# Moving the product with gamma of a layer norm from VectorE to POOL, with a per-row offset for ScalarE, in a two-layer routed adapter kernel

## Chip, cores and metric

One Trainium2 chip, one of its cores. The metric is the device time of one execution in microseconds (us); the median of several runs counts. Before the change it is 2822.74 us (median of 3 runs, 2821.48 to 2826.43).

## What is computed

128 sequences of 128 rows by 1024 columns, in fp32, go through two adapter layers. In each layer a sequence is given one of the layer's adapters by its token `itok`:

```python
h = gelu(x @ W_down[role] + b_down[role])      # 1024 -> 512, exact gelu
u = h @ W_up[role] + b_up[role]                # 512 -> 1024
y = x + u
mean = jnp.mean(y, axis=-1, keepdims=True)
var = jnp.mean(jnp.square(y - mean), axis=-1, keepdims=True)
yn = (y - mean) * rsqrt(var + 1e-5)
out = yn * gamma[role] + beta[role]            # input of the second layer
```

gamma and beta have 1024 values for each adapter, the same for all rows; mean and var are one number for each row.

## The kernel before

**Steps.** At the start VectorE sorts the 128 sequences by adapter and pairs them, so that both sequences of a pair share their weights: 65 pairs a layer, 130 in all. The kernel is a software pipeline over these pairs, one step for each pair `i`. Step `i` runs on every engine and works on several pairs at once: TensorE multiplies pair `i` with W_down (`down`, L492) and pair `u = i-3` with W_up (`product`, L504); `w = i-2` is the pair whose gelu output is transposed and split; `u-1 = i-4` is the pair that is normalised and stored. Within a pair `e` is 0 or 1, the sequence.

**fp32 by three products.** Each operand is split into a high part (ScalarE copies to the rounded type: `high_x` L603, `high_h` L644, `high_wd` L550, `high_wu` L565) and a low part (VectorE subtracts: `low_x` L812, `low_h` L834, `low_wd` L752, `low_wu` L769); TensorE adds high*high, high*low and low*high. W_up is applied to a pair by seven half-size products instead of eight; their inputs are sums that POOL makes (`sums`, L448 to L453, in `cs`). A step has 48 matmuls of `down` and 42 of `product`, all 128x512, in alternation: product 0, down 0, product 1, down 1, and so on, fifteen pieces of six matmuls.

**What VectorE does in a step.** `begin(i)`: transpose the gelu output `hT` (L819), add products 1 and 2 onto the residual `xt` (`onto`, L844), `low_x` of the second sequence, a new adapter's weights if there is one, `low_h(w, 0)`. `end(i)`: `onto` product 3; `variance(u-1)` (L867), a [128, 2] tile from the sums of squares; `scale(u-1, 0)` (L875); in layer 1 `transpose_x` (L805); `low_h(w, 1)`; `last_onto` product 4 (L852); `scale(u-1, 1)`; `last_onto` 5; `low_x` of the next pair; `last_onto` 6; the mean (L860); `low_h(w, 2)`; `last_onto` 7; the mean; `low_h(w, 3)`. TensorE waits on `s_v`, which counts the additions onto `xt`, before it writes a bank again (product 5 waits for addition 4, product 6 for addition 5), and on `s_wd` and `s_wu`, which VectorE's queue signals when a pair's weights stand ready (`ready`, L796).

**The normalisation.** The work on one sequence `xt[:, k, :]` of 128x1024 passes through three engines, each waiting on a semaphore of the one ahead:

```python
scale:  xt = (xt + nmean) * (gamma * sqrt(H))   # VectorE L875, s_n
norm:   rstd = var ** -0.5                      # POOL L433, [128, 2], s_rs
normal: xt = xt * rstd                          # ScalarE L662, waits s_rs, s_n; gives s_z
shift:  xt = xt + beta                          # POOL L440, waits s_z; gives s_o
store:  DMA to mid or out                       # SyncE L338, waits s_o
```

`nmean` is minus the mean. POOL's order in a step is `sums(w)`, `norm(u-1)`, `take_bu` if w has a new adapter (L408, L410), `shift(u-1, 0)`, `factors` if w has a new adapter (L415, L417, L419, three subtractions of 128x1024), `shift(u-1, 1)`, `take_gb` if u has a new adapter (loads gamma and beta to `cgb` and multiplies gamma by sqrt(H), L427).

**What sets the order.** Every engine's instructions stand in a fixed order in its own queue; nothing is scheduled at run time. The steps are loops of six pairs a turn (`steps` for SyncE, VectorE and ScalarE, `plain_steps` for POOL and TensorE), eight turns in each layer, with some steps written out between and around them. `halves` makes a turn of VectorE end after a `begin` and ahead of an `end`, that is ahead of `onto` product 3.

**New adapters.** Pairs are sorted, so the adapter changes four times in all, the first of these at the start. At the other three `take_wd_0`, `take_wd_1` and `take_wu_0` to `take_wu_2` refill the split weights on ScalarE, VectorE and POOL.

Of the kernel before, what the change touches and what calls it, by code (L numbers as in the profile page):

```python
# [46 lines left out]
def routed_adapters(nc, x, xB, itok, Wd, bd, Wu, bu, ga, be, out):  # L47
# [7 lines left out]
    with ctx:  # L55
# [37 lines left out]
        rstd = sb("rstd", [128, 4])  # L93
        mhalf = sb("mhalf", [128, 1])
# [72 lines left out]
        s_n = sem("s_n")  # L167
# [220 lines left out]
        def _(eng):  # L388
# [40 lines left out]
            def norm(p):  # L429
                if p.exists():  # L430
                    n = 2 * (p.c % 2)
                    count(eng, s_var, p, 1, 1)
                    eng.tensor_tensor(rstd[:, n:n + 2], var[:, n:n + 2], mhalf[:, 0:1].broadcast_to([128, 2]), ALU.pow)\  # L433
                       .then_inc(s_rs, 1)

            def shift(p, e):
                if p.exists():
                    k = p.slot(e)
                    count(eng, s_z, p, 2, e + 1)
                    eng.tensor_tensor(xt[:, k, :], xt[:, k, :], cgb[:, 1, :], ALU.add).then_inc(s_o, 1)  # L440
# [101 lines left out]
        def _(eng):  # L542
# [114 lines left out]
            def normal(p, e):  # L657
                if p.exists():
                    n, k = 2 * (p.c % 2) + e, p.slot(e)
                    count(eng, s_rs, p, 1, 1)  # L660
                    count(eng, s_n, p, 2, e + 1)
                    eng.activation(xt[:, k, :], xt[:, k, :], ACT.Copy, scale=rstd[:, n:n + 1]).then_inc(s_z, 1)  # L662
# [34 lines left out]
        def _(eng):  # L697
# [158 lines left out]
            def mean(u, e, n):  # L856
                if u.exists():
                    b = u.c % 2
                    count(eng, s_v, u, 7, n)
                    eng.tensor_scalar(nmean[:, 2 * b + e:2 * b + e + 1], ys[:, b, 2 * e:2 * e + 1],  # L860
                                      ys[:, b, 2 * e + 1:2 * e + 2], -1.0 / H, ALU.add, ALU.mult).then_inc(s_nm, 1)
# [7 lines left out]

            def scale(u, e):  # L870
                if u.exists():
                    n, k = 2 * (u.c % 2) + e, u.slot(e)
                    count(eng, s_sq, u, 4, 2 * e + 2)
                    count(eng, s_cg, u, 1, 1)
                    eng.scalar_tensor_tensor(out=xt[:, k, :], in0=xt[:, k, :], scalar=nmean[:, n:n + 1],  # L875
                                             in1=cgb[:, 0, :], op0=ALU.add, op1=ALU.mult).then_inc(s_n, 1)
# [14 lines left out]
            def end(i):  # L891
# [4 lines left out]
                scale(u + -1, 0)  # L896
# [5 lines left out]
                scale(u + -1, 1)  # L902
# [47 lines left out]
```

## Time and profile before

| | |
|---|---|
| median of 3 runs | 2822.74 us (2821.48 to 2826.43) |
| the profiled execution's own time | 2828.77 us |
| its span | 2826.8 us |
| instructions | 56889 |
| TensorE matmul busy | 2711.9 us (96%) |
| VectorE busy | 2159.2 us (76%) |
| ScalarE busy | 1689.6 us (60%) |
| POOL busy | 1422.4 us (50%) |
| mean granted TensorE clock | 0.982 of full speed |

The span is the time from the first to the last recorded instruction. Rows of a timeline give the start in us from the span's start, then the duration, the engine, the line of the kernel, the operation, output<-inputs, the shapes and how many; in brackets stands how long the engine was idle just before and what ended that. "PE" is TensorE, "DVE" VectorE, "ACT" ScalarE, "SPq" SyncE's queue, "DVEq" VectorE's queue, which handles waits and signals.

### The profile page before, as it was taken

What the parts mean: (1) busy time and instruction counts of PE and PEld (TensorE: products, weight loads), DVE (VectorE), ACT (ScalarE), POOL (GpSimd) and SP (SyncE); (2) the same over time, 40 slices, a digit from 0 to 9 for tenths busy, and PEclk for the clock granted to TensorE, in tenths of its full rate; (3) what the DMA queues carried; (4) which work ended last, traced back from release to release, by engine and by line L of the source; (5) the groups of instructions that cost most, each with busy time, mean ns of one, the idle gap of its engine ahead of it and who ended that gap; (6) DMA issues with size and microseconds to landing.
All of it is one profiled execution on the core that took longest, in us unless ns stands there. A gap on an engine that the chain in (4) does not pass through costs nothing.

```text
span 2826.8 us, 56889 instructions
## 1 busy us (share of the span) xinstructions
PE 2711.9 (96%) x11714; PEld 2216.2 (78%) x11714; DVE 2159.2 (76%) x3321; ACT 1689.6 (60%) x2907; POOL 1422.4 (50%) x956
## 2 busy tenths in 40 slices
PE   7899999998899999999989999999889999999997
PEld 5688888887788888888768888888667888888885
DVE  4677777766777777777788888888787888888886
ACT  3566666565565656666556565666555655656565
POOL 2455555555555555555454444444354444444446
PEclk9999999999999999999999999999999999999999
DMA  6565666666565656666666666656666666666663
GB/s 186 176 202 191 218 205 210 209 222 212 189 209 195 224 197 211 205 207 206 213 200 212 203 207 196 222 192 215 203 197 205 213 199 202 207 192 219 208 203 146
DMA packets 366261, 574.33 MB, mean 203 GB/s; under 512 B 41216, under 2 KB 241024, under 8 KB 365696
## 3 DMA queue, kind: packets, MB, share of 16 engines
q1 hardware_dynamic: 363968, 563.31, 61.5%
q0 software_dynamic: 1728, 6.29, 0.8%
q14 instruction: 553, 4.53, 0.6%
q8 instruction: 12, 0.20, 0.0%
HBM read 364.97 MB, written 204.47 MB: 201 GB/s over the span
## 4 chain that ended last, share of the span: by engine, by line
PE 82%; issue 7%; DVE 5%; POOL 1%; DVEq 1%; ACT 1%; DMA 1%; SPq 1%; POOLq 1%; ACTq 0%
PE pD L492 44%; PE bX L504 22%; PE bZ L504 16%; DVE xt L852 1%; DVE wul L769 1%; DVEq L222 1%; DVE hl L834 1%; DVE xt L875 1%; DVE wdl L752 0%; DVE xt L844 0%; DMA rwd<-in_Wd 0%; DVE xl L812 0%; POOL rwu L408 0%; POOL rwu L415 0%; ACT wdh L550 0%
## 5 line engine op out<-in xcount | busy, mean ns | idle before, releaser
L440 POOL TENSOR_TENSOR xt<-xt,cgb 128x1024 f32<-128x1024 f32 x260 | 699.8, 2692 | 342.9 <-ACT xt L662 341.6
L492 PE MATMUL pD<-wdh,xh 128*128 128x512 f32 x2080 | 818.9, 394 | 48.8 <-DVEq L796 40.4
L492 PE MATMUL pD<-wdl,xh 128*128 128x512 f32 x2080 | 815.1, 392 | 0.0
L492 PE MATMUL pD<-wdh,xl 128*128 128x512 f32 x2080 | 814.1, 391 | 0.0
L662 ACT ACTIVATE xt<-xt,rstd 128x1024 f32<-128x1024 f32 x260 | 298.9, 1150 | 383.1 <-POOL rstd L433 303.0
L492 PEld LDWEIGHTS pD<-wdh,xh 128*128 128x128 f32 x2080 | 394.6, 190 | 140.9 <-DVEq L796 49.5
L492 PEld LDWEIGHTS pD<-wdh,xl 128*128 128x128 f32 x2080 | 394.0, 189 | 83.0
L492 PEld LDWEIGHTS pD<-wdl,xh 128*128 128x128 f32 x2080 | 394.7, 190 | 81.4
L875 DVE SCALAR_TENSOR_TENSOR xt<-xt,nmean,cgb 128x1024 f32<-128x1024 f32 x260 | 441.4, 1698 | 0.0
L448 POOL TENSOR_TENSOR cs<-hT 128x256 f32<-128x256 f32 x130 | 97.1, 747 | 681.7 <-DVE hT L819 679.2
L504 PE MATMUL bX<-wuh,hh 128*128 128x512 f32 x1040 | 410.8, 395 | 27.7 <-DVE xt L844 21.5
L504 PE MATMUL bX<-wul,hh 128*128 128x512 f32 x1040 | 406.9, 391 | 0.0
L504 PE MATMUL bX<-wuh,hl 128*128 128x512 f32 x1040 | 406.9, 391 | 0.0
L644 ACT ACTIVATE hh<-cs 128x512 fp32r<-128x512 f32 x260 | 163.5, 629 | 369.1 <-PE bX L504 303.1
L654 ACT ACTIVATE pC<-xt,nmean 128x512 f32<-128x512 f32 x520 | 358.2, 689 | 41.5 <-issue 18.0
L433 POOL TENSOR_TENSOR rstd<-var,mhalf 128x2 f32<-128x2 f32 x130 | 217.6, 1674 | 315.6 <-DVE var L867 315.5
L504 PE MATMUL bZ<-wuh,hh 128*128 128x512 f32 x780 | 309.8, 397 | 14.7 <-DVE xt L852 13.2
L834 DVE TENSOR_TENSOR hl<-hT,hh 128x256 fp32r<-128x256 f32 (+1 forms) x260 | 157.9, 607 | 212.6 <-issue 151.9
L504 PE MATMUL bZ<-wul,hh 128*128 128x512 f32 x780 | 308.3, 395 | 0.0
L504 PE MATMUL bZ<-wuh,hl 128*128 128x512 f32 x780 | 308.1, 395 | 0.0
L504 PEld LDWEIGHTS bX<-wuh,hh 128*128 128x128 f32 x1040 | 196.1, 189 | 82.3 <-DVE xt L844 30.7
L834 DVE TENSOR_TENSOR hl<-cs,hh 128x512 fp32r<-128x512 f32 x260 | 190.8, 734 | 79.3 <-issue 78.8
(91 smaller groups left out, 3798.8 us busy)
## 6 DMA issues: line engine op xcount, KB each, us to landing
xq<-in_xB SPq DMA_DIRECT2D x130, 512.0 KB, 3.7
htok<-hg SPq DMA_DIRECT2D x260, 256.0 KB, 2.8
hq<-htok SPq DMA_DIRECT2D x1040, 64.0 KB, 2.3
xt<-in_x SPq DMA_DIRECT2D x130, 512.0 KB, 4.2
mid<-xt SPq DMA_DIRECT2D x130, 512.0 KB, 3.9
xq<-mid SPq DMA_DIRECT2D x520, 128.0 KB, 3.2
xt<-mid SPq DMA_DIRECT2D x130, 512.0 KB, 4.1
out<-xt SPq DMA_DIRECT2D x130, 512.0 KB, 2.7
```

The source lines that it names most:

```text
L222: return eng.value_load(c_new[0:1, bass.ds(p.times(1), 1)], min_val=0, max_val=1)
L433: eng.tensor_tensor(rstd[:, n:n + 2], var[:, n:n + 2], mhalf[:, 0:1].broadcast_to([128, 2]), ALU.pow)\
L440: eng.tensor_tensor(xt[:, k, :], xt[:, k, :], cgb[:, 1, :], ALU.add).then_inc(s_o, 1)
L448: eng.tensor_tensor(cs[:, 0, :], b1, b2, ALU.add).then_inc(s_S, 1)
L492: last = eng.matmul(pD[e][:, :], a[:, e, 128 * k:128 * k + 128], w[:, k, :], start=False, stop=(k == 7 and n == 2), skip_group_check=True)
L504: last = eng.matmul(bank[:, :], a[:, left, 128 * c:128 * c + 128], w[:, n, c, :], start=(start and c == 0 and m == 0), stop=(c == 1 and m ...
L644: eng.activation(dst, src, ACT.Copy).then_inc(s_hh, 1)
L654: eng.activation(junk[:, :], xt[:, u.slot(e), K * m:K * m + K], ACT.Square, bias=nmean[:, n:n + 1], accum_out=ssq[:, b, m, e:e + 1]).then_ ...
L662: eng.activation(xt[:, k, :], xt[:, k, :], ACT.Copy, scale=rstd[:, n:n + 1]).then_inc(s_z, 1)
L769: eng.tensor_tensor(wul[:, n, :, :], block, wuh[:, n, :, :].bitcast(fp32), ALU.subtract)\
L834: eng.tensor_tensor(blocks, src, high.bitcast(fp32), ALU.subtract).then_inc(s_hl, 1)
L875: eng.scalar_tensor_tensor(out=xt[:, k, :], in0=xt[:, k, :], scalar=nmean[:, n:n + 1], in1=cgb[:, 0, :], op0=ALU.add, op1=ALU.mult).then_i ...
```

## The change

`scale` leaves VectorE (two instructions a step, and semaphore `s_n`). ScalarE's `normal` becomes `Identity(xt * rstd + nshift)`, where `nshift = nmean * rstd` is a [128, 2] tile that POOL makes right behind `rstd`; it waits for `s_rs` to reach 2 a pair, and for the squares of its sequence (`s_sq`). POOL's `shift` first multiplies the sequence by gamma (128x1024, counted in `s_g`, which the addition of beta waits for) and then adds beta. VectorE's `mean` waits until the `nshift` that reads the same part of `nmean` is done, two pairs back.

```diff
@@ -432,11 +433,17 @@
                     count(eng, s_var, p, 1, 1)
                     eng.tensor_tensor(rstd[:, n:n + 2], var[:, n:n + 2], mhalf[:, 0:1].broadcast_to([128, 2]), ALU.pow)\
                        .then_inc(s_rs, 1)
+                    count(eng, s_rs, p, 2, 1)
+                    eng.tensor_tensor(nshift[:, n:n + 2], nmean[:, n:n + 2], rstd[:, n:n + 2], ALU.mult)\
+                       .then_inc(s_rs, 1)
 
             def shift(p, e):
                 if p.exists():
                     k = p.slot(e)
+                    count(eng, s_cg, p, 1, 1)
                     count(eng, s_z, p, 2, e + 1)
+                    eng.tensor_tensor(xt[:, k, :], xt[:, k, :], cgb[:, 0, :], ALU.mult).then_inc(s_g, 1)
+                    count(eng, s_g, p, 2, e + 1)
                     eng.tensor_tensor(xt[:, k, :], xt[:, k, :], cgb[:, 1, :], ALU.add).then_inc(s_o, 1)
 
             def sums(p):
@@ -657,9 +664,10 @@
             def normal(p, e):
                 if p.exists():
                     n, k = 2 * (p.c % 2) + e, p.slot(e)
-                    count(eng, s_rs, p, 1, 1)
-                    count(eng, s_n, p, 2, e + 1)
-                    eng.activation(xt[:, k, :], xt[:, k, :], ACT.Copy, scale=rstd[:, n:n + 1]).then_inc(s_z, 1)
+                    count(eng, s_rs, p, 2, 2)
+                    count(eng, s_sq, p, 4, 2 * e + 2)
+                    eng.activation(xt[:, k, :], xt[:, k, :], ACT.Identity, bias=nshift[:, n:n + 1],
+                                   scale=rstd[:, n:n + 1]).then_inc(s_z, 1)
 
             eng.wait_ge(s_bits, 1)
 
@@ -857,6 +865,7 @@
                 if u.exists():
                     b = u.c % 2
                     count(eng, s_v, u, 7, n)
+                    count(eng, s_rs, u + -2, 2, 2)
                     eng.tensor_scalar(nmean[:, 2 * b + e:2 * b + e + 1], ys[:, b, 2 * e:2 * e + 1],
                                       ys[:, b, 2 * e + 1:2 * e + 2], -1.0 / H, ALU.add, ALU.mult).then_inc(s_nm, 1)
 
@@ -866,14 +875,6 @@
                     count(eng, s_sq, u, 4, 4)
                     eng.scalar_tensor_tensor(out=var[:, 2 * b:2 * b + 2], in0=ssq[:, b, 0, :], scalar=H * EPS,
                                              in1=ssq[:, b, 1, :], op0=ALU.add, op1=ALU.add).then_inc(s_var, 1)
-
-            def scale(u, e):
-                if u.exists():
-                    n, k = 2 * (u.c % 2) + e, u.slot(e)
-                    count(eng, s_sq, u, 4, 2 * e + 2)
-                    count(eng, s_cg, u, 1, 1)
-                    eng.scalar_tensor_tensor(out=xt[:, k, :], in0=xt[:, k, :], scalar=nmean[:, n:n + 1],
-                                             in1=cgb[:, 0, :], op0=ALU.add, op1=ALU.mult).then_inc(s_n, 1)
 
             def begin(i):
                 u, w = i + -3, i + -2
@@ -893,13 +894,11 @@
                 X = bX[u.c % 2]
                 onto(u, 3, X, 0, 1)
                 variance(u + -1)
-                scale(u + -1, 0)
                 transpose_x(i + 1, 0)
                 low_h(w, 1)
                 when_new(eng, w, take_wu_0)
                 ready(w, s_wu[0])
                 last_onto(u, 4, bZ, 0, 1, 3)
-                scale(u + -1, 1)
                 last_onto(u, 5, X, 1, 1, 2)
                 low_x(i + 1, 0)
                 last_onto(u, 6, bZ, 0, 0, 1)
```

(The declarations of `nshift` and of `s_g` in the place of `s_n` are left out.)

Two places show the order of the instructions. The first is POOL around a pair's `norm`, both `shift`s and a new adapter's `factors` (the three `rwu<-rwu`). Before:

```order
L433 TENSOR_TENSOR rstd<-var,mhalf 128x2
...
L440 TENSOR_TENSOR xt<-xt,cgb 128x1024
...
L415 TENSOR_TENSOR rwu<-rwu 128x2x512
...
L417 TENSOR_TENSOR rwu<-rwu 128x2x512
...
L419 TENSOR_TENSOR rwu<-rwu 128x2x512
...
L440 TENSOR_TENSOR xt<-xt,cgb 128x1024
```

And now, where the lines have moved by one to seven:

```order
L434 TENSOR_TENSOR rstd<-var,mhalf 128x2
L437 TENSOR_TENSOR nshift<-nmean,rstd 128x2
...
L445 TENSOR_TENSOR xt<-xt,cgb 128x1024
L447 TENSOR_TENSOR xt<-xt,cgb 128x1024
...
L416 TENSOR_TENSOR rwu<-rwu 128x2x512
...
L418 TENSOR_TENSOR rwu<-rwu 128x2x512
...
L420 TENSOR_TENSOR rwu<-rwu 128x2x512
...
L445 TENSOR_TENSOR xt<-xt,cgb 128x1024
L447 TENSOR_TENSOR xt<-xt,cgb 128x1024
```

The small product stands directly behind `rstd`, the product with gamma (L445) directly ahead of each addition of beta (L447), and so one of them ahead of the three subtractions for a new adapter's weights.

The second place is VectorE from `onto` product 3 to `last_onto` 5, before:

```order
L844 TENSOR_TENSOR xt<-bX,xt 128x512
L867 SCALAR_TENSOR_TENSOR var<-ssq 128x2
L875 SCALAR_TENSOR_TENSOR xt<-xt,nmean,cgb 128x1024
...
L834 TENSOR_TENSOR hl<-cs,hh 128x512
...
L852 SCALAR_TENSOR_TENSOR xt,ys<-bZ,xt 128x512
L875 SCALAR_TENSOR_TENSOR xt<-xt,nmean,cgb 128x1024
...
L852 SCALAR_TENSOR_TENSOR xt,ys<-bX,xt 128x512
```

Both L875 leave; nothing takes their place, and the rest of VectorE's order stays.

## Rows read from the trace of the kernel before

**Rows 1.** The page: busy time of each engine.
```profile
PE 2711.9 (96%) x11714; PEld 2216.2 (78%) x11714; DVE 2159.2 (76%) x3321; ACT 1689.6 (60%) x2907; POOL 1422.4 (50%) x956
```
**Rows 2.** Timeline of POOL, two steps of layer 1 without a new adapter.
```profile
1908.58 1.68 POOL L433 TENSOR_TENSOR rstd<-var,mhalf 128x2 f32<-128x2 f32 x1 [2.04 <-DVE var L867]
1911.52 2.40 POOL L440 TENSOR_TENSOR xt<-xt,cgb 128x1024 f32<-128x1024 f32 x1 [1.26 <-ACT xt L662]
1916.33 2.40 POOL L440 TENSOR_TENSOR xt<-xt,cgb 128x1024 f32<-128x1024 f32 x1 [2.41 <-ACT xt L662]
1923.45 0.75 POOL L448 TENSOR_TENSOR cs<-hT 128x256 f32<-128x256 f32 x1 [4.71 <-DVE hT L819]
...
1928.98 1.68 POOL L433 TENSOR_TENSOR rstd<-var,mhalf 128x2 f32<-128x2 f32 x1 [2.58 <-DVE var L867]
```
**Rows 3.** Groups of POOL and ScalarE, 1500 to 2770 us: busy us, mean ns | idle before.
```profile
L440 POOL TENSOR_TENSOR xt<-xt,cgb 128x1024 f32<-128x1024 f32 x122 | 294.3, 2413 | 218.9 <-ACT xt L662 218.9
...
L427 POOL TENSOR_TENSOR cgb<-cgb,rooth 128x1024 f32<-128x1024 f32 x1 | 1.9, 1888 | 6.3 <-DMA cgb<-in_be 6.3
...
L662 ACT ACTIVATE xt<-xt,rstd 128x1024 f32<-128x1024 f32 x122 | 140.6, 1153 | 205.5 <-POOL rstd L433 130.8 <-DVE xt L875 74.7
L603 ACT ACTIVATE xh<-xT 128x1024 fp32r<-128x1024 f32 x120 | 121.9, 1016 | 22.6 <-PE pD L492 22.6
```
**Rows 4.** The same view of POOL in layer 0, 100 to 1370 us.
```profile
L440 POOL TENSOR_TENSOR xt<-xt,cgb 128x1024 f32<-128x1024 f32 x121 | 362.8, 2998 | 102.4 <-ACT xt L662 101.1 <-issue 0.3
```
**Rows 5.** Timelines of TensorE and VectorE at a loop turn in layer 1.
```profile
1995.92 0.39 PE L492 MATMUL pD<-wdh,xl 128*128 128x512 f32 x1
1996.91 0.50 PE L504 MATMUL bZ<-wuh,hh 128*128 128x512 f32 x1 [0.60 <-DVE xt L852]
1997.25 0.40 PE L504 MATMUL bZ<-wul,hh 128*128 128x512 f32 x1
...
1993.22 1.28 DVE L875 SCALAR_TENSOR_TENSOR xt<-xt,nmean,cgb 128x1024 f32<-128x1024 f32 x1
...
1996.77 3.10 DVE L875 SCALAR_TENSOR_TENSOR xt<-xt,nmean,cgb 128x1024 f32<-128x1024 f32 x1
```
**Rows 6.** The waits: engine, line waited for: us in total, times, longest us.
```profile
PE pD L492 <- DVEq L796: 40.4, 11, 6.4
...
PE bX L504 <- DVE xt L852: 4.9, 8, 0.6
```
**Rows 7.** Timelines of POOL and VectorE at a loop turn in layer 0.
```profile
1023.77 2.78 POOL L440 TENSOR_TENSOR xt<-xt,cgb 128x1024 f32<-128x1024 f32 x1 [1.34 <-ACT xt L662]
...
1024.80 2.83 DVE L812 TENSOR_TENSOR xl<-xq,xh 128x1024 fp32r<-128x1024 f32 x1
...
1030.00 0.69 DVE L834 TENSOR_TENSOR hl<-cs,hh 128x512 fp32r<-128x512 f32 x1 [1.51 <-issue]
```
**Rows 8.** Timeline of VectorE as a new adapter's W_down, then W_up, is split.
```profile
635.84 1.23 DVE L752 TENSOR_TENSOR wdl<-rwd,wdh 128x1024 fp32r<-128x1024 f32 x1 [0.23 <-DVE wdl L752]
...
720.62 4.54 DVE L769 TENSOR_TENSOR wul<-rwu,wuh 128x1024 fp32r<-128x1024 f32 x3
```
**Rows 9.** Timelines of POOL and TensorE around that W_up.
```profile
705.32 3.38 POOL L415 TENSOR_TENSOR rwu<-rwu 128x1024 f32<-128x1024 f32 x1
...
718.87 0.79 PE L504 MATMUL bX<-wuh,hh 128*128 128x512 f32 x1 [3.40 <-DVE xt L844]
...
726.30 0.79 PE L492 MATMUL pD<-wdh,xh 128*128 128x512 f32 x1 [4.50 <-DVEq L796]
```
**Rows 10.** Timeline of POOL at the kernel's end.
```profile
2780.83 1.68 POOL L433 TENSOR_TENSOR rstd<-var,mhalf 128x2 f32<-128x2 f32 x1 [1.03 <-DVE var L867]
2783.77 5.67 POOL L440 TENSOR_TENSOR xt<-xt,cgb 128x1024 f32<-128x1024 f32 x2 [1.26 <-ACT xt L662]
2791.57 0.73 POOL L448 TENSOR_TENSOR cs<-hT 128x256 f32<-128x256 f32 x1 [2.13 <-DVE hT L819]
...
2818.32 4.64 POOL L440 TENSOR_TENSOR xt<-xt,cgb 128x1024 f32<-128x1024 f32 x2 [1.26 <-ACT xt L662]
```

More of the change, by code:

```diff
@@ L93, in routed_adapters @@
         rstd = sb("rstd", [128, 4])
+        nshift = sb("nshift", [128, 4])
         mhalf = sb("mhalf", [128, 1])
@@ L166, in routed_adapters @@
         s_rs = sem("s_rs")
-        s_n = sem("s_n")
+        s_g = sem("s_g")
         s_z = sem("s_z")
```

## The prediction, made before the changed kernel ran

> **What bounds the kernel.** I read the page first, for the engines' busy time [rows 1], then the timelines of an ordinary step, of a loop turn, of a new adapter and of the end, and ahead of these the list of waits, which says where TensorE stands still. TensorE is busy 96% of the span. An ordinary step takes 20.40 us in both layers (from one `rstd` to the next, 1908.58 to 1928.98 [rows 2]), and TensorE has no gap in it: 90 matmuls, 0.227 us apart (20.40/90). So whatever VectorE gives up in an ordinary step is worth nothing. TensorE stands still in three kinds of places only: at loop turns, where a new adapter's weights are split, and at the end. The change has to be costed there, and it has to be asked whether the longer chain through POOL makes a fourth kind.
>
> **POOL in an ordinary step.** `sums` is four subtractions of 0.75, `rstd` is 1.68, the two `shift`s are 2.40 each [rows 2]: 9.5 us of 20.40. The change adds two products of 128x1024 and `nshift`. The product with gamma has two full inputs like the addition of beta: 2.41, that row's mean [rows 3]. The lower bound is 1.89, the one product POOL does now, which has one full input and one broadcast element [rows 3]; I take 2.41 as the shape is the same. For `nshift`, a [128, 2] product, the bounds are nothing and the 1.68 of the power on the same shape [rows 2]. It is nearest to a 256-wide subtraction with its width taken off: the addition of 1024 costs 2.40 and the subtraction of 256 costs 0.75, so 0.55 for each 256, and 0.2 is left; with the hand-off 0.3. ScalarE's `normal` gets a second per-row operand: one operand more made 1.15 of 1.02 (L662 against L603 [rows 3]), so 0.1 more. POOL then has 9.5+4.8+0.3 = 14.6 us of work, and 1.36 in which it waits for `normal` (1.26 now [rows 2]). From `rstd`'s start the second `shift` ends after 1.68+0.3+1.36+4*2.4+0.2 = 13.1 us, where it now ends after 10.15 (1908.58 to 1918.73 [rows 2]). `sums` of the next step starts 14.87 after `rstd` [rows 2], so 1.7 us of cover are left. The store starts 3 us later, and SyncE's queue behind it too: the store of and the loads for the gelu output, `xq` and `xt`. They are loaded most of a step ahead, so I cost that at nothing; without that cover it would be the same 3 us in every step.
>
> **Who shuts out whom.** Rows 7 show what the sum turns on. VectorE's `low_x` (two inputs in SBUF) began at 1024.80 while POOL's addition ran from 1023.77 to 1026.55, and ended at 1027.63: 2.83 us for what takes 1.2. It got through only when POOL's instruction had ended. In layer 1 `scale(u-1, 1)` took 3.10 instead of 1.28 in the same way [rows 5]. POOL's next instruction waits for VectorE in turn: the additions have a mean of 3.00 in layer 0 [rows 4] and 2.41 in layer 1 [rows 3], where `low_x` reads PSUM. The Trainium skill states this too (GPSIMD Engine Reference, section Key points: POOL shares its SBUF interfaces with VectorE and contends with instructions that have two SBUF inputs). So the change takes two such instructions from VectorE and puts POOL's instructions, at four times 2.4 us back to back, over those that stay: `low_h` (three a step in that stretch), `low_x` in layer 0, and the weight splits L752 and L769.
>
> **Loop turns in layer 1: -14 us.** At a turn VectorE comes back late, and products 5 and 6 wait for additions 4 and 5 [rows 5]. Eight turns, 0.6 us of idle each time [rows 6]. Start to start each stall costs more: 1995.92 to 1996.91 is 0.99 and the next 0.34, against 0.227 each, so 0.76+0.11 = 0.88. Between `onto` 3 and `last_onto` 4 stood 1.28 of `scale`, and ahead of `last_onto` 5 another 3.10 [rows 5]; without them both additions are in time. 8*2*0.88 = 14.1 us.
>
> **Loop turns in layer 0: +12.** There the stalls are small now. After the change the end of the first `shift` moves from 1026.55 to about 1029.3 (a product of 2.4 more and 0.3 of `nshift`), so the next product covers about 1029.4 to 1031.8, just where `low_h(w, 2)` sits (1030.00 [rows 7]), and the last addition covers `low_h(w, 3)` 3 us later. Each can be put off by 0 to 2.4 us; `last_onto` 7, the transposes of `hT` and addition 1 follow, and VectorE is already late there. I take 1.5 us for each of eight turns; bounds 0 and 2.5, so 0 to 20.
>
> **New adapters: +18.** TensorE idles here 40.4 us on `ready` alone [rows 6]. *W_down:* L752 ran at 635.84 in its bare 1.23 [rows 8]; POOL's second `shift` was over. Now a product and an addition still lie ahead of it: up to 2.4 for each of two splits in the first change (in a loop turn of layer 0), less in the others, which fall in layer 1; I take 3.4, 1.6 and 0.8. *W_up:* `factors` stands behind the first `shift`, so L415, at 705.32 [rows 9], starts some 2 to 2.7 us later, and ScalarE's and VectorE's splits of blocks 2 and 3 with it; that reaches TensorE at 718.87 [rows 9]. Then the second `shift`, one product longer, lies under the last three splits, which take 4.54 now against `sums` [rows 8]: another 2 us at 726.30 [rows 9]. 4 us a change, less 0 to 1.3 for the missing `scale`. Together 5.8+12.3 = 18; bounds 5 (VectorE's relief counts in full, half the rest) and 30.
>
> **The end: +13.5.** Here POOL becomes the bound. The last four pairs are normalised with little of TensorE's work between them. Now `rstd` starts at 2780.83, the last addition ends at 2818.32+4.64 = 2822.96 [rows 10]. After the change each pair costs POOL 1.68+0.3+1.36 = 3.3, then four times 2.4 = 9.6, or 12.9, and its order is fixed. First pair: 2780.83+12.9, and 0.9 for what VectorE takes (5.67 for two additions against 4.8 [rows 10]): 2794.6. `sums`, four subtractions of 0.75 [rows 2] and a little for VectorE, 3.1: 2797.7. Three more pairs at 12.9: 2836.4. That is 13.5 more than 2822.96, and the last store follows as now. With 1.89 for a product eight products give back 4: bounds 9 and 16.
>
> **Sum.** -14+12+18+13.5 = +29.5 us. On the profiled execution's 2828.77 that is 2858; on the median of 2822.74, which lies 6 lower, **2852 us**, 1.0% slower.
>
> A rule that speaks against this change: the trace has 2.40 for POOL's addition [rows 2] and 1.28 for VectorE's product with gamma [rows 5]. The Trainium skill's GPSIMD Engine Reference, section Engine selection, says not to put two-input elementwise work on GPSIMD, where it is about twice slower; its Performance section has 4497 ns for 2048 columns. By half of that, 2.25, the end would cost 12 and the sum would be 28.
>
> **The rivals.**
> - *POOL's chain reaches into ordinary steps too.* In layer 0, with 3.0 for each addition [rows 4], POOL's step is 3+1.7+0.3+1.4+4*3.0 = 18.4 and more, near 20.4; the transposes come some 2 us later, `onto` 1 meets the start of product 2, and each of some 100 ordinary steps loses up to 0.7 us. For it: the small reserve of 1.7 us. Against: VectorE loses 2*1.28 us of work a step itself [rows 5], and catches up by that. With 0.5 in 100 steps: 2900 us. Chance 0.2.
> - *VectorE's relief wins* (the other side). The place is the turns and the new adapters. If POOL's longer train lies beside VectorE's two-input work and not over it (each `low_h` slipping into the gap between product and addition, as `low_x` does [rows 7]), layer 0's turns cost nothing, the adapters give back 1.3 at each of six stalls, and the product is 1.89: -14-8+9.5 = -12, or 2810. It decides where a `low_h` waits under 0.3 us on average. Against: the end's 9 us hardly depend on it. Chance 0.1.
> - *A wash:* turns in layer 0 and adapters cost together what is left, 0 to 5: 2818 to 2828. Chance 0.1.
>
> My own forecast (2832 to 2875) has 0.6. A measurement can tell about 0.2%, 5.6 us. Faster by more than that is the second rival alone, 0.1; within it 0.1; slower 0.8. The range takes in the forecast, most of the wash and the first rival up to 2895, from 2820.
>
> **What would show it.** After: L875 is gone and VectorE has some 440 us less (260 instructions, 1.28 to 3.10 each [rows 5]); a product on POOL of 2.4 to 3 us, two a step; `nshift` at 0.2; POOL near 75% busy. In layer 1 no wait of product 5 or 6 for L852 (right or wrong: the -14). At the end POOL's four 128x1024 instructions without a gap, four times, and the last one some 13 us later. TensorE's wait for `ready` up from 40.4. L752 and L769 above 1.23 each. Wrong would be: ordinary steps other than 20.40 us (the first rival), additions by VectorE never behind POOL (the second), or a product on POOL far from 2.4.

## The result, and the profile after

The changed kernel takes 2851.24 us (median of 4 runs, 2847.55 to 2851.66) against 2822.11 (4 runs, 2819.35 to 2826.43): a ratio of 1.0099, 95% interval 1.0081 to 1.0116. It is 1% slower. The forecast was 2852, and that owes much to luck: the two terms for the loop turns were off by 10 and some 15 us in opposite directions, the adapters' sum came out by places other than the forecast named, and of the four terms only the end was near for its own reason.

The page of the changed kernel, and the groups of it that answer to [rows 1, 3, 4]:

```profile
span 2849.0 us, 57199 instructions
...
PE 2706.7 (95%) x11714; PEld 2215.5 (78%) x11714; DVE 1969.1 (69%) x3061; ACT 1709.0 (60%) x2907; POOL 1979.5 (69%) x1346
...
L499 PE MATMUL pD<-wdh,xh 128*128 128x512 f32 x2080 | 818.8, 394 | 60.2 <-DVEq L804 50.0
...
L445 POOL TENSOR_TENSOR xt<-xt,cgb 128x1024 f32<-128x1024 f32 x260 | 641.2, 2466 | 188.5 <-ACT xt L669 187.9
L447 POOL TENSOR_TENSOR xt<-xt,cgb 128x1024 f32<-128x1024 f32 x260 | 698.5, 2686 | 20.4
...
L669 ACT ACTIVATE xt<-xt,nshift,rstd 128x1024 f32<-128x1024 f32 x260 | 322.7, 1242 | 247.5 <-POOL nshift L437 247.5
```

L445 is the new product, L447 the addition (L440 before). POOL has gained 557 us of work, TensorE's wait for `ready` has gone from 40.4 to 50.0. VectorE has lost only 190 us, not the 440 that its L875 took: the other 250 come back as waiting inside its own instructions, `low_h` above all. (In E1 below, where POOL's product is left out, VectorE is busy for 1719.6 us, the whole 440 less.) The same kernel's groups in layer 1, 1500 to 2770 us:

```profile
L842 DVE TENSOR_TENSOR hl<-cs,hh 128x512 fp32r<-128x512 f32 x120 | 168.1, 1401 | 1.6 <-ACT hh L651 1.6
...
L434 POOL TENSOR_TENSOR rstd<-var,mhalf 128x2 f32<-128x2 f32 x60 | 42.5, 708 | 118.2 <-DVE var L876 116.9
L437 POOL TENSOR_TENSOR nshift<-nmean,rstd 128x2 f32<-128x2 f32 x60 | 11.7, 195 | 4.7
```

In the kernel before, this `low_h` takes 0.68 in layer 1; now its mean is 1.40. But `rstd`, which was 1.68 in every step [rows 2], is 0.71.

**Where the time went.** For each kernel I took the start of TensorE's first matmul of every step, and so the length of each of the 130 steps. Here step n is the one in which TensorE multiplies pair n with W_up (`u` = n, so `i` = n+3). The steps fall into groups: the start (to step 1); the ordinary steps and loop turns of each layer; around each of the three new adapters the steps with the split of W_down (27, 62, 92), with the first split of W_up (29, 64, 94), with its other splits (30, 65, 95), and those behind, where gamma and beta are renewed (31, 32, 66, 67, 96, 97); and the end, from step 127 on. The numbers are us more than in the profiled execution of before. "E" are the experiments below; "changed, again" is a second profiled execution of the changed kernel, 2.5 us shorter. One of layer 1's eight loop turns, step 96, falls into "behind"; the column "layer 1" has the other seven.

| | span | start | layer 0 | W_down | W_up 1 | W_up 2 | behind | layer 1 | end |
|---|---|---|---|---|---|---|---|---|---|
| before, length | 2826.8 | 101.5 | 1126.6 | 93.3 | 75.2 | 98.5 | 124.6 | 1094.6 | 51.3 |
| forecast | +29.5 | 0 | +12 | +5.8 | with W_up 2 | +12.3 | 0 | -14 | +13.5 |
| changed | +22.2 | +1.2 | -1.7 | +3.9 | +4.0 | +2.6 | +5.2 | -4.4 | +11.4 |
| changed, again | +19.7 | -2.4 | -4.1 | +4.3 | +5.4 | +2.8 | +6.0 | -3.8 | +11.4 |
| E1 no product | -21.4 | +1.6 | -3.0 | -2.4 | +5.8 | -10.5 | -1.3 | -9.4 | -2.1 |
| E2 both products | +40.6 | +0.7 | +2.3 | +6.5 | +0.7 | +9.1 | +9.4 | -2.1 | +13.8 |
| E3 factors first | +20.4 | +0.5 | -2.7 | +5.0 | +3.8 | +4.2 | +5.9 | -8.4 | +12.2 |
| E4 last four | +14.4 | +1.2 | -3.4 | +4.6 | +4.9 | +5.1 | +4.5 | -3.5 | +1.0 |
| E5 one in six | -4.3 | -1.1 | -0.8 | +3.1 | +6.9 | -6.1 | +2.1 | -10.0 | +1.5 |
| E6 turn pairs | -11.2 | +0.8 | -1.5 | +1.4 | -0.1 | -0.6 | -2.0 | -10.1 | +0.9 |
| E7 offset later | +29.2 | -0.1 | -4.2 | +2.8 | -1.3 | +12.2 | +8.1 | 0.0 | +11.8 |
| E9 gamma late | +12.4 | -1.6 | -2.5 | +4.9 | +3.7 | +5.0 | -0.4 | -8.3 | +11.6 |

(Steps 28, 63 and 93 are 20.40 everywhere, 20.51 once in E2, and left out.) Between the two executions of the changed kernel the start moves by 3.6 us and single groups by up to 2.4; smaller differences than that say nothing. All rows are taken against one execution of before, which itself took 2828.77 us, 5 to 7 above that kernel's medians. So in all rows but E2's the span lies 2 to 7 us below the difference of the medians (E5: -4.3 here, +1.8 by its medians); in which groups those us lie can't be told.

**An ordinary step** of the changed kernel, POOL in layer 1, beside [rows 2]:

```profile
1607.06 0.70 POOL L434 TENSOR_TENSOR rstd<-var,mhalf 128x2 f32<-128x2 f32 x1 [1.78 <-DVE var L876]
1607.84 0.20 POOL L437 TENSOR_TENSOR nshift<-nmean,rstd 128x2 f32<-128x2 f32 x1
1609.46 2.40 POOL L445 TENSOR_TENSOR xt<-xt,cgb 128x1024 f32<-128x1024 f32 x1 [1.43 <-ACT xt L669]
1611.93 2.42 POOL L447 TENSOR_TENSOR xt<-xt,cgb 128x1024 f32<-128x1024 f32 x1
1614.31 2.40 POOL L445 TENSOR_TENSOR xt<-xt,cgb 128x1024 f32<-128x1024 f32 x1
1616.78 2.39 POOL L447 TENSOR_TENSOR xt<-xt,cgb 128x1024 f32<-128x1024 f32 x1
```

From `rstd`'s start to the last addition's end it is 12.1 us, where I had worked out 13.1; the difference is `rstd`. `sums` follows at 1622.71, 3.5 us later. That gap is not cover: `low_h` is held until the addition has ended (below, 1617.66), and an addition, the mean, another `low_h` and the transposes follow it on VectorE almost without a break, up to `sums`. So POOL's longer train now sets when `sums` starts, 3.1 us into an ordinary step of layer 1 (2.3 before) and 3.4 in layer 0 (2.0 before). In layer 0 there is less room still. In the second and third step behind most turns POOL has no break at all between the last addition and `sums`; step 10 starts at 287.40:

```profile
290.22 2.75 POOL L447 TENSOR_TENSOR xt<-xt,cgb 128x1024 f32<-128x1024 f32 x1
293.31 1.35 POOL L455 TENSOR_TENSOR cs<-hT 128x256 f32<-128x256 f32 x1 [0.34 <-issue]
```

`sums` starts 5.9 us into it. TensorE loses at most 0.25 us there (20.40 to 20.65), and its ordinary steps stay 20.40 in both layers, so the first rival did not come.

### The profile page after: what moved, and what is told of

It reads as the page before. It is cut to its first block, busy times and chain, and to the rows that moved or that the text cites. A ratio compares the mean times of both kernels' runs of the same rounds, so it can differ in the third digit from the quotient of the medians.

```text
span 2849.0 us, 57199 instructions
## 1 busy us (share of the span) xinstructions
PE 2706.7 (95%) x11714; PEld 2215.5 (78%) x11714; DVE 1969.1 (69%) x3061; ACT 1709.0 (60%) x2907; POOL 1979.5 (69%) x1346
## 4 chain that ended last, share of the span: by engine, by line
PE 75%; issue 8%; POOL 5%; DVE 4%; ACT 2%; DMA 1%; DVEq 1%; SPq 1%; POOLq 1%; ACTq 0%
PE pD L499 40%; PE bX L511 20%; PE bZ L511 15%; POOL xt L445 2%; DVE hl L842 1%; DVEq L223 1%; DMA rwd<-in_Wd 1%; DVE wul L777 1%; DVE wdl L760 1%; DVE xt L860 1%; POOL xt L447 1%; POOLq L474 1%; ACT xt L669 1%; DVE xt L852 0%; ACT xh L610 0%
## 5 line engine op out<-in xcount | busy, mean ns | idle before, releaser
L445 POOL TENSOR_TENSOR xt<-xt,cgb 128x1024 f32<-128x1024 f32 x260 | 641.2, 2466 | 188.5 <-ACT xt L669 187.9
L447 POOL TENSOR_TENSOR xt<-xt,cgb 128x1024 f32<-128x1024 f32 x260 | 698.5, 2686 | 20.4
L669 ACT ACTIVATE xt<-xt,nshift,rstd 128x1024 f32<-128x1024 f32 x260 | 322.7, 1242 | 247.5 <-POOL nshift L437 247.5
L842 DVE TENSOR_TENSOR hl<-cs,hh 128x512 fp32r<-128x512 f32 x260 | 350.6, 1349 | 82.6 <-issue 56.3
L455 POOL TENSOR_TENSOR cs<-hT 128x256 f32<-128x256 f32 x130 | 107.4, 826 | 389.1 <-DVE hT L827 358.1
L860 DVE SCALAR_TENSOR_TENSOR xt<-bX,xt 128x512 f32<-128x512 f32 x260 | 178.4, 686 | 214.9 <-PE bX L511 208.5
L511 PE MATMUL bZ<-wuh,hh 128*128 128x512 f32 x780 | 307.9, 395 | 14.4 <-DVE xt L860 12.1
L842 DVE TENSOR_TENSOR hl<-hT,hh 128x256 fp32r<-128x256 f32 (+1 forms) x260 | 224.9, 865 | 113.9 <-issue 92.4
L860 DVE SCALAR_TENSOR_TENSOR xt<-bZ,xt 128x512 f32<-128x512 f32 x260 | 179.1, 689 | 153.9 <-PE bZ L511 151.3
```

Of the source, the lines that this page charges most:

```text
L445: eng.tensor_tensor(xt[:, k, :], xt[:, k, :], cgb[:, 0, :], ALU.mult).then_inc(s_g, 1)
L455: eng.tensor_tensor(cs[:, 0, :], b1, b2, ALU.add).then_inc(s_S, 1)
L511: last = eng.matmul(bank[:, :], a[:, left, 128 * c:128 * c + 128], w[:, n, c, :], start=(start and c == 0 and m == 0), stop=(c == 1 and m ...
L669: eng.activation(xt[:, k, :], xt[:, k, :], ACT.Identity, bias=nshift[:, n:n + 1], scale=rstd[:, n:n + 1]).then_inc(s_z, 1)
L842: eng.tensor_tensor(blocks, src, high.bitcast(fp32), ALU.subtract).then_inc(s_hl, 1)
L860: eng.scalar_tensor_tensor(out=half(u, e, m), in0=bank[:, :], scalar=1.0, in1=half(u, e, m), op0=ALU.mult, op1=ALU.add, accum_out=ys[:, b, ...
```

## The experiments

**E1, the changed kernel without the product.** gamma is not applied, so the time is that of a kernel that does less.

```diff
                     count(eng, s_z, p, 2, e + 1)
-                    eng.tensor_tensor(xt[:, k, :], xt[:, k, :], cgb[:, 0, :], ALU.mult).then_inc(s_g, 1)
-                    count(eng, s_g, p, 2, e + 1)
                     eng.tensor_tensor(xt[:, k, :], xt[:, k, :], cgb[:, 1, :], ALU.add).then_inc(s_o, 1)
```

> The changed kernel with POOL's product with gamma left out (gamma is not applied): VectorE's relief without POOL's longer train. My account (the gain in layer 1 is eaten by POOL's train holding up VectorE's low_h): both stalls at the eight loop turns of layer 1 go, -14 us, a few us less at the end, about 2804 us. Rival (the gain was never there, since the late VectorE at a turn moves the stall to the wait ahead): the turns keep some 1.2 us each and the time stays at 2812 to 2820. Rival 2 (the new waits on nshift cost something): above 2822.

Measured: 2806.06 us (2805.49 to 2807.51) against 2824.15, ratio 0.9935 (0.9918 to 0.9951). VectorE's relief alone, with `nshift` already paid, is worth 18 us; the product on POOL then costs 45 (43 against E8). The table says where: against E1 the changed kernel loses 6 us at W_down, 13 at the second part of W_up, 6.5 behind the adapters, 5 in layer 1, 13.5 at the end. Of these places only the first W_up split does not improve in E1 (+5.8): that one belongs to `nshift`, below.

**E2, the kernel before with the product added.** VectorE's `scale` stays, so gamma is applied twice.

```diff
                     count(eng, s_z, p, 2, e + 1)
+                    eng.tensor_tensor(xt[:, k, :], xt[:, k, :], cgb[:, 0, :], ALU.mult).then_inc(s_g, 1)
+                    count(eng, s_g, p, 2, e + 1)
                     eng.tensor_tensor(xt[:, k, :], xt[:, k, :], cgb[:, 1, :], ALU.add).then_inc(s_o, 1)
```

> The kernel before with POOL's product with gamma added and VectorE's left in place (gamma is applied twice): POOL's train without VectorE's relief. If POOL's instructions only make POOL's own queue longer, it costs the end (+13) and new adapters (+4 to +8): about 2842 us. If they also shut VectorE out of its instructions with two SBUF inputs, VectorE's work grows from 16.6 us a step to over 20 and ordinary steps get longer than 20.40 us: 2860 to 2920 us.

Measured: 2863.63 us (2861.83 to 2869.09), ratio 1.0137 (1.0120 to 1.0154). That lies in the range for two engines in each other's way, but the step it was to come by did not come: VectorE is busy for 2267.4 us against 2159.2, and yet its ordinary steps stay at 20.40 to 20.47. The exceptions are steps 10, 16, 34, 40 and 58 in layer 0, each two behind a turn, at 20.95 to 22.25: there TensorE waits up to 1.56 us for a signal that stands in VectorE's queue. The loss is again at the adapters (+25.7 in four groups) and at the end. Groups of its POOL in layer 1, 1500 to 2770 us:

```profile
L443 POOL TENSOR_TENSOR xt<-xt,cgb 128x1024 f32<-128x1024 f32 x119 | 361.1, 3034 | 9.3
L441 POOL TENSOR_TENSOR xt<-xt,cgb 128x1024 f32<-128x1024 f32 x119 | 286.3, 2406 | 74.8 <-ACT xt L665 74.8
...
L434 POOL TENSOR_TENSOR rstd<-var,mhalf 128x2 f32<-128x2 f32 x60 | 99.6, 1659 | 78.9 <-DVE var L870 77.1
```

With `scale` back, `rstd` is back at 1.66, and the addition is at 3.03 where [rows 3] have 2.41.

**E4, the changed kernel with the last four pairs scaled by VectorE**, as before (`on_pool` stands around the product, in `normal` and around `scale`):

```diff
+        def on_pool(p):
+            return p.j is not None or p.c < NPH - 4
```

> The changed kernel, the last four pairs scaled by VectorE as before: if the end is bound by POOL's eight more products, it gives back the 11 us of the end, 2840 us against 2851. If the end was longer for another reason (later stores, ScalarE), 2849 or more.

Measured: 2840.13 us (2838.30 to 2842.89), ratio 1.0054 (1.0037 to 1.0071). The end falls from +11.4 to +1.0 and the time by 11 us against the changed kernel's 2851.24; the other groups stay within 2.5 us of the changed kernel's. The end's term is its own. POOL's timeline at the end of the changed kernel, beside [rows 10]:

```profile
2808.27 1.15 POOL L434 TENSOR_TENSOR rstd<-var,mhalf 128x2 f32<-128x2 f32 x1
2809.50 0.20 POOL L437 TENSOR_TENSOR nshift<-nmean,rstd 128x2 f32<-128x2 f32 x1
2811.12 2.38 POOL L445 TENSOR_TENSOR xt<-xt,cgb 128x1024 f32<-128x1024 f32 x1 [1.42 <-ACT xt L669]
...
2821.78 0.70 POOL L434 TENSOR_TENSOR rstd<-var,mhalf 128x2 f32<-128x2 f32 x1 [0.19 <-DVE var L876]
...
2833.87 0.70 POOL L434 TENSOR_TENSOR rstd<-var,mhalf 128x2 f32<-128x2 f32 x1 [0.19 <-issue]
...
2843.39 2.34 POOL L447 TENSOR_TENSOR xt<-xt,cgb 128x1024 f32<-128x1024 f32 x1
```

The last two pairs are 12.1 us apart, POOL without a gap but for the wait for `normal`. I had 12.9 a pair.

**E5, the product on POOL for one pair in six**, in layer 1 the pairs that are normalised at the loop turns; VectorE scales the others, and `nshift` is made for all:

```diff
+        def on_pool(p):
+            return p.c % 6 == 5
```

> The kernel before, with POOL's product for one pair in six, the one that is normalised at the loop turns of layer 1; VectorE scales all others, nshift is made for all. If the gain of the changed kernel at these turns is lost because the pair ahead leaves VectorE late, it is whole here: -14 us, 2808 us. If POOL's train within the turn itself takes it, each turn keeps about 1.2 us of stall: 2818 us.

Measured: 2825.92 us (2823.66 to 2829.72), ratio 1.0009 (0.9999 to 1.0018). Both of my numbers were too low. The table shows part of it: layer 1 gains 10 us of the 14 expected, and W_up 1 loses 6.9; `nshift` is in every step here (E7). The pair with the product also falls on a new adapter (step 31: 23.17 us).

**E6, the same only for every sixth pair of layer 1, and `nshift` for those alone:** eleven pairs, among them the eight that are normalised at a loop turn. POOL's steps are looped as VectorE's are here, a second difference to the kernel before.

```diff
+        def on_pool(p):
+            return p.layer() == 1 and (p.c - NP) % 6 == 0
```

> The kernel before, with POOL's product and nshift only for the ten or so pairs of layer 1 that are normalised at its loop turns (POOL's steps are written out and looped as VectorE's are). The turns of layer 1 give 11 us as with one pair in six, and what that version lost in layer 0 and at new adapters stays away: 2812 us, 0.4% faster than before. If the loss there came from somewhere else than from nshift and products in other steps, 2820 or more.

Measured: 2816.40 us (2811.59 to 2818.22, 7 runs) against 2824.10, ratio 0.9968 (0.9957 to 0.9980). This version is 0.3% faster than the kernel before and so beats both. Layer 1 gains 10.1 us, as in E5, where POOL's loop is as before, so the new loop isn't what gives them; the eighth turn gives 1.8 more (in "behind"). The largest loss is 2.4 us at the third new W_down, which the last part of this text comes back to. Its trace also shows the two forms side by side. POOL, a step before the turn and the turn, and VectorE's `scale` (L906) beside the first:

```profile
1594.52 1.68 POOL L447 TENSOR_TENSOR rstd<-var,mhalf 128x2 f32<-128x2 f32 x1 [2.20 <-DVE var L898]
...
1594.35 1.28 DVE L906 SCALAR_TENSOR_TENSOR xt<-xt,nmean,cgb 128x1024 f32<-128x1024 f32 x1
...
1618.20 0.70 POOL L447 TENSOR_TENSOR rstd<-var,mhalf 128x2 f32<-128x2 f32 x1 [5.76 <-DVE var L898]
1618.98 0.20 POOL L451 TENSOR_TENSOR nshift<-nmean,rstd 128x2 f32<-128x2 f32 x1
```

The first pair is scaled by VectorE, and its 1.28 us with two inputs lie over `rstd`; the second is not. The same instruction, 24 us later in the same kernel, takes 0.70 instead of 1.68. So 1 us of `rstd` was waiting.

**Why layer 1 gains 10 here and 4 in the changed kernel.** VectorE at a loop turn, first of the changed kernel (the step starts at 1619.62), with TensorE's stall:

```profile
1617.66 2.08 DVE L842 TENSOR_TENSOR hl<-cs,hh 128x512 fp32r<-128x512 f32 x1
...
1621.33 1.30 DVE L827 STREAM_TRANSPOSE hT<-hq 128x512 f32<-128x512 f32 x2
...
1630.86 0.69 DVE L852 TENSOR_TENSOR xt<-bX,xt 128x512 f32<-128x512 f32 x1 [4.00 <-issue]
...
1631.61 0.50 PE L511 MATMUL bX<-wuh,hh 128*128 128x512 f32 x1 [0.91 <-DVE xt L852]
```

and of E6 (the step starts at 1607.08):

```profile
1605.71 0.67 DVE L862 TENSOR_TENSOR hl<-cs,hh 128x512 fp32r<-128x512 f32 x1
...
1608.08 1.31 DVE L847 STREAM_TRANSPOSE hT<-hq 128x512 f32<-128x512 f32 x2
...
1617.36 0.69 DVE L872 TENSOR_TENSOR xt<-bX,xt 128x512 f32<-128x512 f32 x1 [3.44 <-PE bZ L526]
```

The stalls of products 5 and 6 [rows 5] are gone in both; in the changed kernel one at product 4 took their place. VectorE comes back from the turn with `onto` 3 at 11.24 into the step instead of 10.28, and TensorE waits 0.91 for that. The seven turns last 21.2 to 21.7 us, against 22.2 to 22.4 before and 20.5 to 20.8 in E6. In all kernels without `scale` at these turns the turn's length is `onto` 3's start plus some 10.4 us.

It looks as if the `low_h` of 1617.66 did it: it starts under POOL's addition of 1616.78, takes 2.08 until that has ended, and the transposes come 0.7 us later in the step. The other traces speak against that. The first turn of layer 1 (step 72), in us from the step's start:

| | `low_h` ahead takes | transposes at | `low_h(w, 0)` at | VectorE idle at the turn | `onto` 3 at |
|---|---|---|---|---|---|
| changed | 2.08 | 1.71 | 6.82 | 4.00 | 11.24 |
| E1 | 0.67 | 0.18 | 6.79 | 3.15 | 10.36 |
| E3 | 2.33 | 1.81 | 6.52 | 3.65 | 10.60 |
| E6 | 0.67 | 1.01 | 6.42 | 3.44 | 10.28 |
| E9 | 2.52 | 1.90 | 6.51 | 3.42 | 10.36 |

In E3 and E9 `low_h` is held longer than in the changed kernel, and `onto` 3 is still 0.6 to 0.9 earlier; in E1 the transposes are 1.5 us earlier and `low_h(w, 0)` starts at the same time. So a delay of the transposes is not what arrives at `onto` 3. What is longer in the changed kernel is above all VectorE's idle time at the turn itself, between `low_h(w, 0)` and `onto` 3: 3.7 to 4.2 over the seven turns of both executions, against 3.3 to 3.7 in E3 and 3.2 to 3.5 in E6. What sets that time, no run shows, and so the cause of layer 1's missing 6 us stays open.

**E7, `nshift` behind the new adapter's first work on POOL.** In the changed kernel's queue `nshift` stands ahead of L409, which makes the block of W_up that the first stall waits for. Here it stands behind `take_bu`.

```diff
+                offset(u + -1)          # nshift, taken out of norm
                 shift(u + -1, 0)
```

> The changed kernel with nshift issued behind the look at the new adapter's flag and what follows it. If POOL's queue, held by the wait for rstd, is what puts off the first subtraction for W_up by 1.3 us, the first stall of each of three new adapters shrinks by that: 2847 us. If it is nshift's own duration or another wait, 2850 to 2853. In ordinary steps nothing changes on TensorE.

Measured: 2858.21 us (2856.73 to 2858.93), ratio 1.0120 (1.0104 to 1.0135): 7 us worse than the changed kernel's 2851.24 and 9 worse than its 2849.27 in E8, where I had expected 4 better. The step that it was made for does what was expected: W_up 1 goes from +4.0 or +5.4 to -1.3. Over the whole table that group is +3.7 to +6.9 in each kernel with `nshift` ahead of L409, and -1.3 to +0.7 in the three without (E2, E6, E7). POOL's timeline of the changed kernel in that step:

```profile
694.56 1.16 POOL L434 TENSOR_TENSOR rstd<-var,mhalf 128x2 f32<-128x2 f32 x1 [0.45 <-DVE var L876]
695.80 1.17 POOL L437 TENSOR_TENSOR nshift<-nmean,rstd 128x2 f32<-128x2 f32 x1
698.03 0.62 POOL L406 DMA_DIRECT2D cbu<-in_bu  x1 [1.06 <-issue]
698.67 2.39 POOL L409 TENSOR_TENSOR rwu<-rwu 128x1024 f32<-128x1024 f32 x1
```

and of E7, with TensorE's stalls:

```profile
690.94 1.16 POOL L434 TENSOR_TENSOR rstd<-var,mhalf 128x2 f32<-128x2 f32 x1 [0.37 <-DVE var L881]
693.20 0.62 POOL L406 DMA_DIRECT2D cbu<-in_bu  x1 [1.11 <-issue]
693.85 2.41 POOL L409 TENSOR_TENSOR rwu<-rwu 128x1024 f32<-128x1024 f32 x1
...
699.70 0.50 PE L516 MATMUL bZ<-wuh,hh 128*128 128x512 f32 x1 [2.83 <-DVE xt L865]
...
719.95 0.80 PE L516 MATMUL bX<-wuh,hh 128*128 128x512 f32 x1 [7.00 <-DVE xt L857]
```

`nshift`, 0.20 in an ordinary step, takes 1.17 here (VectorE's split L777 runs beside it). From `rstd`'s start to L409's it is 4.11 with it, 2.91 without. But now `nshift`, and with it `normal` and both shifts, stands behind the wait for the adapter's bias, and the second stall grows from 4.57 to 7.00 (W_up 2: +12.2). And in layer 1 the step after each turn is 21.4 us instead of 20.7. I had priced what the move frees and not what it delays.

**E3, `factors` in part ahead of the first shift.** The subtractions L416 and L418 don't stand behind the product any more:

```diff
+                when_new(eng, w, factors_early)    # L416, L418
                 shift(u + -1, 0)
-                when_new(eng, w, factors)
+                when_new(eng, w, factors_late)     # L420
```

> The changed kernel with two of the three subtractions for a new adapter's W_up ahead of POOL's first product with gamma. If that product ahead of them is what costs 2 to 3 us at each of three new adapters, it gives back 2 us at each, less what one more look at the adapter's flag costs: 2845 us against 2851. If VectorE being shut out is the cost there, nothing changes: 2849 to 2852.

Measured: 2847.85 us (2846.51 to 2849.24), ratio 1.0082 (1.0067 to 1.0098). Between the two expectations, and within the scatter of the changed kernel (2849.27 in E8). The adapters' groups do not improve (W_up 2 is +4.2 against +2.6 and +2.8). That does not clear the order: the delay was there, and moving it away brought another in its place. ScalarE's copies and VectorE's splits of the next two blocks of W_up, first of the changed kernel, then of E3; in both step 30 starts at 713.0 or 713.1:

```profile
713.76 2.01 ACT L572 ACTIVATE wuh<-rwu 128x1024 fp32r<-128x1024 f32 x2 [4.75 <-POOL rwu L416]
714.85 3.57 DVE L777 TENSOR_TENSOR wul<-rwu,wuh 128x1024 fp32r<-128x1024 f32 x2 [3.38 <-ACT wuh L572]
```

```profile
708.80 2.01 ACT L578 ACTIVATE wuh<-rwu 128x1024 fp32r<-128x1024 f32 x2
710.33 6.76 DVE L783 TENSOR_TENSOR wul<-rwu,wuh 128x1024 fp32r<-128x1024 f32 x2
```

In the changed kernel ScalarE waits 4.75 for L416 (13.0 in all at the four adapters, against 5.6 before and 0.7 in E1). In E3 it starts 5 us earlier, but now POOL's first product and addition lie over the two splits, which take 6.76 instead of 3.57. The few us of E3 come from layer 1, where the turns are 20.6 to 21.1 instead of 21.2 to 21.7. E9 has the same, and both have one more look at a flag in POOL's queue ahead of the first shift. Why that helps I can't show.

**E8, the changed kernel again.**

> The changed kernel once more, on the same chip as these, as the yardstick for them and for the gap between the profiled spans (22 us) and the medians (29 us): 2851 us if the medians are right, 2846 if the spans are.

Measured: 2849.27 us (2846.50 to 2855.39) against 2824.10, ratio 1.0094 (1.0078 to 1.0110). The two medians lie 2 us apart, so less than that between kernels is not to be read.

**E9, the wait for gamma and beta one step later.** The table showed a group that the forecast did not have, behind the adapters. POOL issues the loads of gamma and beta in the changed kernel only behind four 128x1024 instructions instead of two, and then its queue waits. POOL at the first change, and TensorE's longest stall behind the second:

```profile
756.30 1.89 POOL L428 TENSOR_TENSOR cgb<-cgb,rooth 128x1024 f32<-128x1024 f32 x1 [7.02 <-DMA cgb<-in_be]
758.69 0.73 POOL L455 TENSOR_TENSOR cs<-hT 128x256 f32<-128x256 f32 x1 [0.51 <-issue]
...
1522.93 0.50 PE L511 MATMUL bX<-wuh,hh 128*128 128x512 f32 x1 [1.81 <-DVE xt L852]
```

Here the `sums` of step 31 start 10.6 us into the step (it starts at 748.07). Before it was 6.0, which was already 3 us later than in step 32, and TensorE did not notice. In E9 the wait and L428 stand in the next step, behind `rstd`:

```diff
+                v = u + -1
+                if v.exists():
+                    when_new(eng, v, ready_gb)      # the wait and L428
+                    eng.drain().then_inc(s_cg, 1)
                 shift(u + -1, 0)
```

> The changed kernel, with POOL's wait for the new adapter's gamma and beta, and its scaling of gamma, put off to the next step, behind sums and rstd and ahead of the first shift. It bears on a place that the prediction did not have: behind a new adapter's gamma and beta. In the changed kernel POOL issues these loads two products later, waits 7 us for them, and the sums of the next pair start 10.6 us into the step where they started 6.0 before; TensorE then loses time in the four or five steps behind each change (21.75 and 21.09, 20.93 and 22.51, 22.49 and 21.03 us in one execution, against 20.40 and 20.74, 20.40 and 20.40, 22.27 and 20.40 before). If the wait in POOL's queue is what does it, these six steps lose some 5 us together, the sums start under 6 us into the step, and the time is 2845 (2843 to 2847). If the steps are long only because POOL's and VectorE's work is itself late after the weights' splits, they stay as they are, and the time is 2849 to 2852. A cost is possible: one more look at a flag in each step, ahead of the first shift; where the same look stood there in another run, the ordinary steps stayed at 20.40.

Measured: 2842.69 us (2841.32 to 2844.43, 5 runs) against 2822.88, ratio 1.0068 (1.0055 to 1.0082). "Behind" goes from +5.2 or +6.0 to -0.4; steps 32, 66 and 67 are 20.40 again. POOL's timeline of E9 (step 31 starts at 745.20):

```profile
745.81 0.53 POOL L426 DMA_DIRECT2D cgb<-in_be  x1
748.06 0.74 POOL L457 TENSOR_TENSOR cs<-hT 128x256 f32<-128x256 f32 x1 [1.72 <-DVE hT L832]
```

`sums` starts 2.9 us into the step. (In the group's -0.4 is 0.5 that the turn of step 96 gains.) The place is shown, and its 5 to 6 us; the rest of the 6.6 to 8.6 us gained is layer 1's turns, as in E3.

## Why the prediction was right, and where it was not

**The sign and the size: right.** The profile's lines for VectorE and POOL gave it: POOL's product is 2.47 (2.41 forecast), it does bind at the end, and VectorE's freed time is worth something at few places. But the sum was made against a profiled execution that lay 6 us above its kernel's median, and the changed kernel's profiled executions lay on or 1 us below theirs. Span against span the change costs 22.2 or 19.7 us, not 29.5; median against median 29.1 or 25.2. The forecast's 2852 owes 6 us to that. And within the sum two errors cancel: the turns of layer 1 gave 10 us less than forecast, those of layer 0 cost 14 to 16 less.

**The end, +13.5: right, a little large.** 11.4 twice, and E4 gives it back. The step "each pair costs POOL 1.68+0.3+1.36" was off in its first number: `rstd` is 0.70 to 1.15 once VectorE's `scale` is gone. I had read 1.68 as the price of a power of 128x2; it was a price and a wait, though [rows 7] had already told me that POOL waits for VectorE. E6 shows it within one trace.

**Loop turns in layer 1, -14: mechanism right, size a third.** Products 5 and 6 wait no more. The step "without them both additions are in time" held only for additions 4 and 5; it did not ask for `onto` 3, which comes at 10.7 to 11.2 us into the step, with VectorE idle for 3.7 to 4.2 ahead of it, and became the stall. -4.4 and -3.8 measured for seven of the eight turns; the eighth gave -0.3 at best (22.27 before, 22.49 and 21.99 after). E6 gets 10.1 and E1 9.4, but E3 and E9, with POOL's whole train in place, get 8.4 and 8.3: the train's length is not what takes the 6 us, and what does is open.

**Loop turns in layer 0, +12: wrong.** -1.7 and -4.1. The step "`low_h(w, 2)` and `low_h(w, 3)` can be put off by 0 to 2.4 us each" is what happens (the mean of the `low_h` with `cs` is 1.27 in layer 0, 0.73 before), and the transposes start 2.0 us into a turn where they started at 0.6, about the 1.5 that I took. What failed is the next step, "VectorE is already late there": `low_h(w, 0)` starts at 6.2 in the changed kernel as before, so the delay is gone before VectorE reaches the turn and does not get to TensorE. The turns are 20.4 to 21.5 us and the steps behind them 20.40, where they were 20.4 to 20.9 and 20.7 to 20.8; what is left of the difference between turns is again VectorE's idle time there, 2.5 to 4.3. Even E2, where VectorE keeps its `scale`s too, has only +2.3.

**New adapters, +18: 15.7 and 18.5, in good part by another route.** W_down is +3.9 and +4.3 against 5.8, but not where I had it. For the three adapters in turn I had 3.4, 1.6 and 0.8; it was 1.1, -0.6 and 3.4 (1.3, -0.1 and 3.1 again). At the first two VectorE's splits L760 are shut out as forecast (up to 3.06 for 1.23). At the third, where the loss is, they are not: each takes its bare 1.22 or 1.23. There the step that failed is the one on SyncE's queue behind the later store, "so I cost that at nothing": it named the loads of the gelu output, `xq` and `xt`, and not those of the weights. SyncE issues them in step 91, 13.5 us behind the second store of the pair normalised in step 90, before, after and in E6 alike, and that store now waits for POOL's longer train (it is issued 3.1 us into step 91, where it was issued 1.0 ahead of it). SyncE's issue and ScalarE's copy of the first half, before:

```profile
2017.16 1.85 SPq L267 DMA_DIRECT2D rwd<-in_Wd  x4
...
2023.83 2.01 ACT L550 ACTIVATE wdh<-rwd 128x1024 fp32r<-128x1024 f32 x2 [1.11 <-DMA rwd<-in_Wd]
```

and in the changed kernel:

```profile
2028.89 1.85 SPq L268 DMA_DIRECT2D rwd<-in_Wd  x4
...
2035.57 2.00 ACT L557 ACTIVATE wdh<-rwd 128x1024 fp32r<-128x1024 f32 x2 [6.11 <-DMA rwd<-in_Wd]
```

The issue is 12.4 us into step 91 before and 16.8 after, and ScalarE waits 6.11 for the landing instead of 1.11. E6 has the same (16.5 us, a wait of 3.97, and the 2.4 us lost), from the product of the one pair ahead; E1, without any product, has 13.4.

W_up is 6.6 and 8.2 against 12.3. The delay of `factors` behind the first product came (L416 starts 2.2 us ahead of step 30, L415 4.6 ahead before) and so did the cost of the product, 13 us against E1; E3 shows only that another order pays the same elsewhere. What I mis-sized is VectorE's relief, 0 to 1.3 a change: E1 gains 10.5 there, 3.5 a change. And `nshift` ahead of L409, which I had at 0.3 us, costs the first stall 4 to 5 us over the three changes (E7). To this come 5 to 6 us behind the adapters, which I had at nothing (E9). I had checked each instruction that POOL's queue delays against TensorE's waits of before; here none stood before, since 3 us of delay in `sums` were still covered, and so the place was not in the list.

**Ordinary steps, 0: right,** though not by the cover of 1.7 us that I worked out: `sums` is later in every step, by 0.8 us in layer 1, 1.4 in layer 0 and up to 4.2 two steps behind a turn, and TensorE still has its inputs in time. The first rival (0.2) fell; its picture of a full POOL came true in some steps of layer 0 without the price. **VectorE's relief wins** (0.1) did not come for the whole kernel, but it does where the product is kept to a few pairs: that is E6.

The Trainium skill's GPSIMD Engine Reference (sections Specifications and Engine selection) speaks of contention between POOL and VectorE where VectorE reads two inputs from SBUF, and against two-input work on POOL. The traces agree with both: 0.67 became 2.08 for a `low_h` under POOL's addition, and the product is 2.47 where VectorE took 1.28.

## What to carry to other kernels

Moving an instruction to an idle engine is priced where the two engines meet, not by its length: list what the longer train will lie over, and also what was lying over the engine's own instructions before, since a duration in the trace can be half wait. Follow each queue past the last place where the kernel stands still today; a wait that was still covered (gamma and beta) becomes a stall when the train ahead of it grows by 5 us. Follow also the queue that only stores and loads: a store that waits longer holds the weight loads behind it. And a change that loses as a whole can win at eight loop turns of 130 steps.

## What I had not expected of the hardware

The exclusion works on the smallest instructions. A power of 128x2 on POOL takes 0.70 us alone and 1.68 beside a VectorE instruction with two SBUF inputs; a product of the same shape takes 0.20 alone and 1.17 at a new adapter's step, beside the split of its weights. Each ends only once the other engine's instruction has ended, and two of them by the same margin: in E6 VectorE's `scale` ends at 1595.63 and the 1.68 us `rstd` at 1596.20; in the changed kernel POOL's addition ends at 1619.17 and `low_h` at 1619.74, 0.57 us later both times.
